# Sweeps of a recurrence with one coefficient and one gated input operation for both row blocks of a unit

## The reference

```python
def step(h_prev, zt_gt):
    z_t, g_t = zt_gt
    gate = jax.nn.sigmoid(z_t @ Wgz + bgz + h_prev @ Wgh + bgh)
    h_tilde = (1.0 - gate) * h_prev + gate * z_t
    h_t = h_tilde + g_t * h_prev
    return (h_t, h_t)
```

## Time and profile before

| | us |
|---|---|
| median of three executions | 1104.19 |
| profiled execution | 1103.62 |
| its span | 1101.8 |
| TensorE busy | 916.7 (83%) |
| VectorE busy | 572.0 (52%) |
| ScalarE busy | 420.0 (38%) |
| GpSimd busy | 47.9 (4%) |
| sweeps 1 to 5 on VectorE (101.54 to 202.46) | 100.92 |
| checking sweep on VectorE (202.46 to 238.4) | 35.9 |

### The profile page before, as it was taken

One profiled execution on the slowest core, in us unless ns is written; L12 is line 12 of the kernel. 1 busy time (PEld: TensorE's weight loads), 2 busy tenths in 40 slices (PEclk: granted clock), 3 DMA queues, 4 the chain that ended last, 5 costly groups with the idle time before them and its releaser, 6 DMA issues.

```text
span 1101.8 us, 11446 instructions
## 1 busy us (share of the span) xinstructions
PE 916.7 (83%) x4572; PEld 437.7 (40%) x4572; DVE 572.0 (52%) x817; ACT 420.0 (38%) x526; POOL 47.9 (4%) x39
## 2 busy tenths in 40 slices
PE   3995799659899989976699988968888997886978
PEld 2532344233344334354225336223365445632332
DVE  3378999963301330245715135157579485944352
ACT  4462222344312432163161532636721374123434
POOL 0000000300000000000300000000011001100000
PEclk8898999868899889966889995979989898987999
DMA  8000000000000000110000000000000000000001
GB/s 354 1 0 0 1 0 0 0 1 1 0 1 0 1 1 0 39 68 1 1 1 1 1 0 2 1 1 15 1 1 1 0 1 1 1 1 1 11 28 38
DMA packets 3435, 15.78 MB, mean 14 GB/s; under 512 B 832, under 2 KB 1344, under 8 KB 2752
## 3 DMA queue, kind: packets, MB, share of 16 engines
q1 hardware_dynamic: 3248, 13.07, 3.1%
q0 software_dynamic: 144, 2.10, 0.5%
HBM read 12.67 MB, written 2.10 MB: 13 GB/s over the span
## 4 chain that ended last, share of the span: by engine, by line
PE 55%; DVE 25%; ACT 10%; issue 8%; DMA 1%; DVEq 0%; POOLq 0%; SPq 0%; POOL 0%; ACTq 0%
PE ps L368 54%; DVE AR L1490 3%; DVE AR L1491 3%; ACT AR L573 2%; DVE AR L1493 2%; DVE AR L1623 1%; DVE VB L584 1%; DVE AR L1773 1%; DVE AR L1760 1%; DVE AR L462 1%; DVE AR L1764 1%; DMA CX<-in_ctxT 1%; DVE AR L1769 1%; DVE AR L456 1%; DVE VB L1493 1%
## 5 line engine op out<-in xcount | busy, mean ns | idle before, releaser
L368 PE MATMUL ps<-AR,WA 128*128 128x512 f32 (+3 forms) x808 | 363.5, 614 | 20.8 <-DVE AR L462 6.0
L368 PEld LDWEIGHTS ps<-AR,WA 128*128 128x128 f32 (+2 forms) x808 | 154.4, 196 | 225.2 <-issue 192.7
L368 PE MATMUL ps<-AR,CN 128*128 128x512 f32 (+3 forms) x336 | 135.5, 666 | 37.8 <-DVE AR L459 21.7
L368 PE MATMUL ps<-AR 128*64 128x128 f32 (+5 forms) x680 | 105.3, 440 | 11.7 <-DVE AR L1762 5.3
L368 PEld LDWEIGHTS ps<-AR,CN 128*128 128x128 f32 (+2 forms) x336 | 47.0, 182 | 101.3 <-issue 52.4
L592 DVE TENSOR_TENSOR AR<-ps,AR 128x512 f32<-128x512 f32 x24 | 16.6, 692 | 119.9 <-ACT AR L578 119.9
L368 PEld LDWEIGHTS ps<-AR 128*64 128x64 f32 (+4 forms) x680 | 53.4, 171 | 51.6 <-issue 17.8
L584 DVE TENSOR_REDUCE VB<-ps 128x16 f32<-128x1232 f32 x32 | 45.1, 1440 | 45.8 <-PE ps L368 45.8
L573 ACT ACTIVATE AR<-ps 77x2048 f32<-77x2048 f32 x24 | 44.0, 1869 | 62.4 <-PE ps L368 62.4
L1564 DVE SCALAR_TENSOR_TENSOR X<-ps,VC,X 128x512 f32 x8 | 5.6, 747 | 108.3 <-PE ps L368 108.3
L368 PE MATMUL ps<-KF,AR 32*128 32x77 f32 x1024 | 45.3, 341 | 12.3 <-ACT AR L1254 5.2
(11 more groups left out here) (263 smaller groups left out, 1071.1 us busy)
## 6 DMA issues: line engine op xcount, KB each, us to landing
WA<-in_m SPq DMA_DIRECT2D x1, 2856.0 KB, 10.3
WA<-in_m SPq DMA_DIRECT2D x1, 2560.0 KB, 15.7
X<-in_xT POOLq DMA_DIRECT2D x1, 2048.0 KB, 9.4
WA<-in_m SPq DMA_DIRECT2D x1, 2048.0 KB, 20.6
out<-X SPq DMA_DIRECT2D x4, 512.0 KB, 3.1
WB<-in_m SPq DMA_DIRECT2D x1, 1024.0 KB, 22.4
AR<-in_rows SPq DMA_DIRECT2D x1, 640.0 KB, 10.1
WA<-in_m SPq DMA_DIRECT2D x1, 512.0 KB, 16.5
```

Source lines behind the costliest of these rows:

```text
L368: return nc.tensor.matmul(out, lhsT, rhs, start=first, stop=last)
```

## The change

In the five sweeps that are not checking, VectorE forms the coefficient of both row blocks in one instruction of 1024 columns, and the gated input of both in another, and then scans the two row blocks one after the other, each with 512 columns as before. The tiles UG, GZ and AA are laid out as one block `UGB[b]`, `GZB[b]`, `AAB[b]` of (2, 512) per sequence, with the old names as views of it. The wait for the gates moves in front of the first subtraction and asks for both gates of the unit. The checking sweep keeps its instructions. All semaphores count as before.

```diff
-        UG = [[c1.take(T) for _ in range(DC)] for _ in range(B)]
-        GZ = [[c1.take(T) for _ in range(DC)] for _ in range(B)]
-        AA = [[c1.take(T) for _ in range(DC)] for _ in range(B)]
+        UGB, GZB, AAB = ([c1.take(DC, T) for _ in range(B)] for _ in range(3))
+        UG, GZ, AA = ([[a[:, mo, :] for mo in range(DC)] for a in both] for both in (UGB, GZB, AAB))
...
+                        if not checking:
+                            half = slice(jj * T, (jj + 1) * T)
+                            dve.wait_ge(*after("g", nk(j, 8, 2 * q - 1)))
+                            TT(AAB[b], OPG[:, :, b, half], UGB[b], ALU.subtract)
+                            ch.link(TT(GZB[b], UGB[b], Z[:, :, b, half], ALU.mult))
                         for mo in range(DC):
                             k = 2 * (q - 1) + mo
+                            if not checking:
+                                first = dst[:, mo, b, 0, T * jj:T * jj + 1]
+                                nc.vector.tensor_tensor_scan(dst[:, mo, b, jj, span], AA[b][mo], GZ[b][mo],
+                                                             first, ALU.mult, ALU.add).then_inc(sem("h"), 1)
+                                continue
                             dve.wait_ge(*after("g", nk(j, 8, k)))
                             TT(AA[b][mo], OPG[:, mo, b, jj * T:(jj + 1) * T], UG[b][mo], ALU.subtract)
                             ch.link(TT(GZ[b][mo], UG[b][mo], Z[:, mo, b, jj * T:(jj + 1) * T], ALU.mult))
                             first = dst[:, mo, b, 0, T * jj:T * jj + 1]
-                            scan = nc.vector.tensor_tensor_scan(UG[b][mo] if checking else dst[:, mo, b, jj, span], AA[b][mo], GZ[b][mo],
-                                                                first, ALU.mult, ALU.add)
-                            if not checking:
-                                scan.then_inc(sem("h"), 1)
-                                continue
+                            scan = nc.vector.tensor_tensor_scan(UG[b][mo], AA[b][mo], GZ[b][mo], first, ALU.mult, ALU.add)
                             ch.link(scan)
```

## The result

The changed kernel takes 1093.57 us in the median of 22 runs (1087.87 to 1098.17), the kernel before 1102.57 in 22 runs beside it (1095.96 to 1104.79). The ratio is 0.9918, with a 95% interval of 0.9902 to 0.9934: 9.0 us faster, where 4.8 were forecast. With the runs that came beside the experiments the kernel before has 143, with a mean of 1101.6 (standard error 0.2); one more, of 1820.8 us, is left out. The change has a mean of 1093.4 (0.7). In means the gain is 8.2 us; with the 22 runs beside the change alone (mean 1102.5, error 0.5) it is 9.1. The profiled execution of the change took 1089.79 us (span 1088.0), 13.8 less than that of before, so it is a lucky one, and it must not be read as the whole effect.

The account below looks back on a forecast made before the run. VectorE was taken to bound the sweeps' 20 units: 1.12 + 1.255 + 1.20 + 1.20 = 4.775 us each, saving 0.238 a unit, 4.8 us in all, so 1099.4 us from a median of 1104.19. The 8-in-10 range was 1097.8 to 1101.9.

Parts of the forecast that it names:

- VectorE bounds the sweeps and TensorE has a lead: In the five edited sweeps VectorE sets the pace; TensorE's lead at the checking sweep shrinks from 7.8 to 4.2 us.
- The sum of a unit: VectorE's start-to-start distances in one sweep unit: 1.12 + 1.255 + 1.20 + 1.20 = 4.775 us, against 5.01 before.
- Scan behind scan: Distance between starts of a unit's two scans on VectorE: taken as 1.20 us, with bounds 1.18 and 1.32.
- The wait for both gates and the later first result: In each sweep unit, waiting for both gates and getting the first scan's result 1.2 us later cost nothing.
- The first rival: In the sweeps a scan starts only after the one before ends: 1.284 or 1.32 us, total 1101.1 or 1101.8; chance 0.10.
- The second rival: From the third sweep TensorE's 5.15 us a unit sets the pace: only 1.2 us gained, 1103.0; chance 0.07.
- The third rival: TensorE's low granted clock falls onto the third sweep: if onto all of it, 11.6 us later, 1115.8; chance 0.05.
- so all 4.8 us reach the end: Behind the sweeps, count and flag hang on VectorE's checks, so the sweeps' whole 4.8 us saving shortens the execution.
- stages behind may move by a few tenths as they start at another time: Stages after the sweeps shift by only tenths of a us; part of the forecast's own range, 1098.2 to 1100.8.

## Why the prediction was wrong

By its own steps:

- VectorE bounds the sweeps and TensorE has a lead: right. No wait on a gate appeared. The lead came out at 2.1 us instead of 4.2: the slow first passes of the third sweep took 1.4 of it, and VectorE's earlier arrival 0.7.
- The sum of a unit: right but for one term. Scan behind scan is 1.18 apart, the bound below, and not 1.20. Forecast 4.775 a unit and 4.8 us for the stage (checking sweep at 197.7, less 0.2 for an earlier start); measured 4.75, or 4.81 with the copy, and 5.26. That is 0.46 more than forecast, of which 0.4 is 0.02 in each of 20 units.
- The wait for both gates and the later first result cost nothing: right.
- The first rival (a scan behind a scan costs 1.284 or 1.32) is refuted by 1.18. The Trainium skill's rule for it, "VectorE: DVE Perf Modes", section "The DRAIN you can't avoid", would have made the pair 2.57 us long; the trace has 2.46, so it disagrees with the rule; the section itself adds that a next operation that isn't held starts earlier, and that is what the trace shows. The second rival is refuted too.
- The third rival named the right thing at the wrong place: the low clock did fall onto the third sweep, and cost nothing there. What was said against it, that TensorE's pauses get shorter, held for two of them (1.81 and 2.06 us); the one ahead of the third sweep grew from 0.88 to 1.99.
- **The step that failed** is "so all 4.8 us reach the end", with "stages behind may move by a few tenths as they start at another time". The stages behind the sweeps don't have a fixed length. At the place of the kernel before they cost 2.6 us more in the mean than at that of the change (1101.6 against 1093.4, less 5.6; error 0.7, and with the changed kernel delayed by 5.6 us, 2.6 with an error of 1.0). The delays show it: the changed kernel put back by 5.6 us takes 1101.6, and put back by only 1.2 us takes 1099.3.
- The 0.37 us between flag and attention weren't forecast. With narrow instructions the wait there is 5.19, with wide ones 4.83 or 4.84, also in the delayed kernels. ScalarE's wait for VectorE's sequencer behind the flag holds all of it (2.71 instead of 3.07); what in the code makes it wasn't tried.

The sum of the means: 5.26 in the sweeps, 0.37 at the flag, and 2.6 by the place of the later stages, 8.2 in all. That the place acts by TensorE's granted clock is shown in so far as time and clock go together over the runs, the windows of slow and fast traces differ in it, and keeping TensorE busy moved both. In the two profiled executions, 8.0 us apart behind the attention's start, 3.2 us arise within the first five exponentials of the second layer and the rest in several smaller pieces; since these two differ by more than the means do, that says where time can be lost and not how the 2.6 us divide. What moves the steps of the clock from run to run, so that runs of one kernel differ by up to 10 us, stays open as well.

The range was too narrow for a reason that could be seen: three runs that spread 2.0 us were taken for the kernel's spread, while 22 runs spread 8.8. They also gave a base of 1104.19, 1.6 above the median of the 22, so that the forecast of 1099.4 misses 1093.57 by 5.8 us, of which 1.6 are the base. The page of before has the granted clock between five and nine tenths from slice to slice up to the end, so the length of stages bound by TensorE was open to begin with.

## What to carry to other kernels

Price a chain on VectorE by the distances between starts, each with its own kind of neighbour, and take a short pair of the same kind for a pair that the trace doesn't have; that was good to 1% of a unit (4.775 against 4.75), though the saving, a small difference of such sums, came out 10% larger (5.26 against 4.8). Then don't stop at the edited stage: where TensorE's granted clock changes over a span and TensorE bounds later stages, the same shift can be worth very different times. Here a start earlier by 5.6 us was worth 8.2 us between delays of 5.6 and 0, and 0.3 (error 1.0) between delays of 6.8 and 1.2. Compare such kernels by the means of many runs, and test with plain delays at the same place before the excess is put down to the edit.

## What the runs showed of the hardware

- Runs of one kernel on one core spread over 9 to 10 us (1095.96 to 1104.79 before, 1087.87 to 1098.17 after, 22 runs each), and in the change their time goes with TensorE's mean granted clock (correlation -0.89).
- Two scans of 512 columns back to back start 1.18 us apart at a duration of 1.28; a subtraction behind a scan starts after 1.20.
- Products without use in TensorE's pauses, together with half of the queries moved into one, made the whole 3.5 to 4.2 us faster where they covered the three pauses up to the attention. Covering only the first of the three gave nothing that could be told (ratio 1.0006, 0.9978 to 1.0035).
- VectorE's f32 operation on 863 columns took 1.06 us alone (5.42 for five in a chain). Beside GpSimd's pass over the weights five took 6.99, and the longest of them 1.85.
